# Moving the transposed adjacency of seven batches to its ring by DMA, and new orders on all five queues

## What is computed

```
v, q, k = relu(x Wv + bv), relu(x Wq + bq), relu(x Wk + bk)
att     = softmax((q k^T) * adj - 9e15 * (1 - adj))          # over the last axis
x1      = layernorm(x + relu((att v) Wo + bo))
h       = x1 W_w^T + W_b
u       = adj * exp((h a1)[:, None] + (h a2)[None, :] + a_b)
out     = layernorm(x1 + (u / sum(u)) h)
```

## Time and profile before

| | us |
|---|---|
| median of three runs | 395.15 (395.12 to 395.23) |
| the profiled execution | 395.13 |
| its span, first to last instruction | 393.4 |
| PE busy | 380.5 (97%) |
| ACT busy | 329.9 (84%) |
| DVE busy | 292.8 (74%) |
| POOL busy | 279.9 (71%) |

### The profile page before, as it was taken

The page is one execution under the profiler, slowest core; times in us unless marked ns, Lnnn a source line. Parts: engine busy times, 40 slices in busy tenths (PEclk is TensorE's granted clock), DMA queues, the critical chain, the costliest instruction groups (busy, mean ns, idle before and its releaser), DMA issues.

```text
span 393.4 us, 8653 instructions
## 1 busy us (share of the span) xinstructions
PE 380.5 (97%) x2757; PEld 355.2 (90%) x2757; DVE 292.8 (74%) x883; ACT 329.9 (84%) x661; POOL 279.9 (71%) x258
## 2 busy tenths in 40 slices
PE   8999999999999999999999999999999999999990
PEld 7798989989999999999999999999999999999990
DVE  3786796678668886777957887688867779697976
ACT  5877679987889887997879878898888969999962
POOL 1454951696458994789937998389956899576673
PEclk9999999999999999999999999999999999999996
DMA  8945533807657168754597266780676647978011
GB/s 259 376 166 166 164 129 137 328 38 268 200 185 314 61 235 260 262 203 171 175 292 298 84 240 215 243 322 13 253 214 233 252 162 285 386 224 282 4 55 53
DMA packets 38156, 80.71 MB, mean 205 GB/s; under 512 B 2785, under 2 KB 19681, under 8 KB 38113
## 3 DMA queue, kind: packets, MB, share of 16 engines
q1 hardware_dynamic: 37824, 80.03, 58.3%
q10 hardware_dynamic: 288, 0.14, 0.1%
HBM read 75.96 MB, written 4.19 MB: 204 GB/s over the span
## 4 chain that ended last, share of the span: by engine, by line
PE 91%; DVE 5%; issue 2%; POOL 0%; ACT 0%; POOLq 0%; DVEq 0%; ACTq 0%
PE pt_ps L1612 14%; PE m_ps L1660 13%; PE s_ps L1541 8%; PE av_ps L1625 8%; PE av_ps L1626 8%; PE av_ps L1624 8%; PE s_ps L1543 7%; PE s_ps L1542 7%; PE m_ps L1583 4%; PE m_ps L1649 3%; PE m_ps L1633 3%; PE m_ps L1541 2%; PE m_ps L1542 2%; PE m_ps L1543 2%; PE m_ps L1640 2%
## 5 line engine op out<-in xcount | busy, mean ns | idle before, releaser
L1033 DVE TENSOR_TENSOR prob_tl<-pt_ps,prob_th 128x512 fp32r<-128x512 f32 x128 | 85.5, 684 | 29.8 <-ACT prob_th L670 29.6
L1025 DVE CUSTOM_DVE_ANT_0 prob<-s_ps,penalty 128x1024 f32<-128x1024 f32 x64 | 78.0, 1218 | 30.8 <-PE s_ps L1543 26.2
L670 ACT ACTIVATE prob_th<-pt_ps 128x512 fp32r<-128x512 f32 x128 | 74.7, 596 | 21.0 <-PE pt_ps L1612 20.8
L405 POOL TENSOR_SCALAR penalty<-raw 128x1024 bf16<-128x1024 f32 x64 | 66.4, 1047 | 28.3 <-DMA raw<-in_adj_dram 13.2
L662 ACT ACTIVATE prob<-prob,neg_max 128x1024 f32<-128x1024 f32 x64 | 73.8, 1153 | 1.4 <-DVE neg_max L1025 1.3
L1624 PE MATMUL av_ps<-prob_th,vh 128*128 128x256 f32 x256 | 74.1, 290 | 0.0
L1612 PE MATMUL pt_ps<-rhs,prob 128*128 128x128 f32 x512 | 73.2, 273 | 0.0
L1626 PE MATMUL av_ps<-prob_th,vl 128*128 128x256 f32 x256 | 72.4, 283 | 0.0
L1625 PE MATMUL av_ps<-prob_tl,vh 128*128 128x256 f32 x256 | 72.4, 283 | 0.0
L607 ACT ACTIVATE adj_t<-adjt_in 128x1024 fp32r<-128x1024 f32 x56 | 59.3, 1061 | 11.2 <-PE m_ps L1660 11.1
L1612 PEld LDWEIGHTS pt_ps<-rhs,prob 128*128 128x128 f32 x512 | 60.1, 141 | 4.1
(11 more groups left out here) (139 smaller groups left out, 785.2 us busy)
## 6 DMA issues: line engine op xcount, KB each, us to landing
raw<-in_adj_dram SPq DMA_DIRECT2D x64, 512.0 KB, 5.6
adjt_in<-in_adj_t_dram SPq DMA_DIRECT2D x56, 512.0 KB, 3.9
x_in<-in_x_dram SPq DMA_DIRECT2D x8, 512.0 KB, 6.2
raw<-in_adj_t_dram SPq DMA_DIRECT2D x8, 512.0 KB, 5.7
out_dram<-out_sb SPq DMA_DIRECT2D x14, 256.0 KB, 4.5
xt_odd<-in_x_t_dram SPq DMA_DIRECT2D x8, 256.0 KB, 5.2
raw<-in_x_t_dram SPq DMA_DIRECT2D x7, 256.0 KB, 4.7
out_dram<-out_sb SPq DMA_DIRECT2D x4, 128.0 KB, 1.8
```

The lines of the kernel that those rows point to most:

```text
L670: sc.activation(prob_th[n % 2][:, tiles(k), (i % 2) * P:(i % 2 + 1) * P], pt_ps[k][:, :].rearrange("p (c n) -> p c n", n=P), ACT.Copy).the ...
L1025: v.tensor_tensor_reduce(out=prob[i % 2][:, :], in0=s_ps[:, :, :].rearrange("p a n -> p (a n)"), in1=penalty[:, n % RING, :], scale=-1.0, ...
L1033: v.tensor_tensor(prob_tl[n % 2][at], pt_ps[k][:, :].rearrange("p (c n) -> p c n", n=P), prob_th[n % 2][at].bitcast(F32), ALU.subtract).th ...
```

## The change

The transposed tiles of batches 0 to 6 are no longer copied from staging to ring by ACT. SP issues a DMA from the staging buffer to the ring buffer instead, behind a wait for the aggregate that frees the ring buffer and a wait for the tile's own load. Its end is what the aggregate and the next load into that staging buffer wait for, on one semaphore for each ring buffer. The bits are moved as they are. `round_adj` is gone from ACT's lists. All lists of the five queues have a new order, and so have the three lists of PSUM banks; no other step is added or left out. Of the orders those are shown that the text speaks of; in the rest only steps change places.

```diff
-        adjt_done = sem("adjt_done")
+        adjt_done = [sem(f"adjt_done{r}") for r in range(RING)]
...
             def load_adj_t(b, i):
                 n = T * b + i
-                wait(sp, adjt_done, n - STAGING + 1)
+                if n >= STAGING:
+                    sp.wait_ge(adjt_done[(n - STAGING) % RING], 16 * ((n - STAGING) // RING + 1))
                 sp.dma_start(adjt_in[:, n % STAGING, :, :], adj_t_tiles[b, i]).then_inc(adjt_arrived[n % STAGING], 16)
+
+            def copy_adj_t(b, i):
+                n = T * b + i
+                wait(sp, agg_full, n - RING + 1)
+                sp.wait_ge(adjt_arrived[n % STAGING], 16 * (n // STAGING + 1))
+                sp.dma_start(flat(adj_tile(b, i)).bitcast(F32), flat(adjt_in[:, n % STAGING, :, :])).then_inc(adjt_done[n % RING], 16)
 
...
             def head():
+                load_x_t(0, 1)
                 load_x_t_quarter(0)
                 load_x_t_quarter(1)
-                load_x_t(0, 1)
                 load_wb()
+                load_x_t(2, 0)
                 load_adj(0, 0)
+                load_x_t(1, 0)
                 load_adj(0, 1)
-                load_x(0)
-                load_x_t(1, 0)
-                load_x_t(1, 1)
...
             def batch_pass(p):
                 if there(p - 2):
+                    load_adj_t(p - 2, 6)
+                if there(p - 2):
                     load_adj_t(p - 2, 5)
+                if there(p - 2):
+                    copy_adj_t(p - 2, 6)
+                if there(p - 2):
+                    copy_adj_t(p - 2, 5)
                 load_adj(p, 4)
-                if there(p - 2):
-                    load_adj_t(p - 2, 6)
+                if there(p - 3):
+                    store(p - 3, 0)
                 load_adj(p, 5)
+                if there(p - 2):
+                    load_adj_t(p - 2, 7)
+                load_adj_t(p - 1, 0)
+                if there(p - 2):
+                    copy_adj_t(p - 2, 7)
+                if there(p + 2):
+                    load_x_t(p + 2, 1)
+                load_adj(p, 6)
+                load_adj_t(p - 1, 1)
+                copy_adj_t(p - 1, 0)
+                load_adj(p, 7)
+                load_adj(p + 1, 0)
+                load_adj_t(p - 1, 2)
+                copy_adj_t(p - 1, 2)
                 if there(p + 2):
                     load_x_t(p + 2, 0)
-                if there(p - 2):
-                    load_adj_t(p - 2, 7)
-                load_adj_t(p - 1, 0)
-                if there(p - 3):
-                    store(p - 3, 0)
-                if there(p + 2):
-                    load_x_t(p + 2, 1)
+                copy_adj_t(p - 1, 1)
+                load_adj_t(p - 1, 3)
+                load_adj(p + 1, 1)
                 if there(p - 3):
                     store(p - 3, 1)
-                load_adj_t(p - 1, 1)
+                copy_adj_t(p - 1, 3)
+                load_adj_t(p - 1, 4)
+                load_adj(p + 1, 3)
+                load_adj(p + 1, 2)
                 load_x(p + 1)
-                load_adj_t(p - 1, 2)
-                load_adj(p, 6)
-                load_adj(p, 7)
-                load_adj_t(p - 1, 3)
-                load_adj(p + 1, 0)
-                load_adj(p + 1, 1)
-                load_adj(p + 1, 2)
-                load_adj(p + 1, 3)
-                load_adj_t(p - 1, 4)
+                copy_adj_t(p - 1, 4)
 
...
             def batch_pass(p):
+                if there(p - 2):
+                    g_lo(p - 2, 0)
                 convert(p, 1)
                 if there(p - 2):
-                    g_lo(p - 2, 0)
-                if there(p - 2):
                     g_lo(p - 2, 1)
-                x_lo(p + 1, 0)
+                if there(p - 3):
+                    rstd1_pow(p - 3)
...
-            def round_adj(b, i):
-                n = T * b + i
-                wait(act, agg_full, n - RING + 1)
-                act.wait_ge(adjt_arrived[n % STAGING], 16 * (n // STAGING + 1))
-                sc.activation(flat(adj_tile(b, i)), flat(adjt_in[:, n % STAGING, :, :]), ACT.Copy).then_inc(adjt_done, 1)
...
             def head():
                 first_x_hi(0)
                 first_x_hi(1)
+                q_out(0, 0)
                 x_hi(0, 1)
-                q_out(0, 0)
                 k_out(0, 0)
+                v_relu(0, 0)
+                k_hi(0, 0)
                 q_hi(0, 0)
-                k_hi(0, 0)
                 k_out(0, 1)
+                v_relu(0, 1)
                 k_hi(0, 1)
+                v_relu(0, 2)
                 q_out(0, 1)
                 x_hi(1, 0)
...
             def head():
-                split_in(0)
                 first_x_lo_quarter(0)
                 first_x_lo_quarter(1)
+                split_in(0)
                 split_in(1)
+                centre_w()
+                v_bias(0, 0)
+                place_rhs1()
                 first_x_lo(1)
-                place_rhs1()
-                centre_w()
                 first_k_lo(0)
+                v_bias(0, 1)
                 first_q_lo(0)
-                v_bias(0, 0)
                 first_k_lo(1)
-                v_bias(0, 1)
+                v_bias(0, 2)
                 mask_max(0, 0)
-                v_bias(0, 2)
                 v_bias(0, 3)
                 v_bias(1, 0)
...
                 stats0_pair(2)
+                g_lo_pair(0)
+                stats1(LAST - 1, 0)
+                mean_var0_pair(2)
+                mean_var1(LAST - 1, 0)
+                inverse_sum_pair(3)
+                o_out(LAST, 3)
+                var_eps0_pair(2)
+                residual0(LAST, 3)
+                stats1(LAST - 1, 1)
                 shift0_pair(1)
-                mean_var0_pair(2)
-                stats1(LAST - 1, 0)
-                g_lo_pair(0)
-                mean_var1(LAST - 1, 0)
-                var_eps0_pair(2)
-                g_lo_den_pair(0)
-                stats1(LAST - 1, 1)
-                o_out(LAST, 3)
                 mean_var1(LAST - 1, 1)
-                residual0(LAST, 3)
+                var_eps1(LAST - 1)
...
                     pe.wait_ge(gl_done, 2 * (b + 1))
-                pe.wait_ge(adjt_done, n + 1)
+                pe.wait_ge(adjt_done[n % RING], 16 * (n // RING + 1))
...
                 first_project_q(0)
                 first_project_q(1)
                 project_k(0, 0)
+                project_v(0, 0)
+                project_v(0, 1)
                 project_k(0, 1)
                 project_q(0, 1)
-                project_v(0, 0)
                 form_w1()
-                project_v(0, 1)
+                project_v(0, 2)
                 first_scores(0)
                 first_scores(1)
-                project_v(0, 2)
                 project_v(0, 3)
                 project_v(1, 0)
+                project_v(1, 1)
                 scores(0, 1)
                 transpose_p(0, 0, 0)
...
             def batch_pass(p):
                 scores(p, 0)
                 transpose_p(p - 1, 7, 0)
+                if there(p - 2):
+                    aggregate(p - 2, 0)
                 transpose_p(p - 1, 7, 1)
                 project_out(p - 1, 1)
                 project_out(p - 1, 2)
                 scores(p, 1)
+                if there(p - 2):
+                    aggregate(p - 2, 1)
                 transpose_p(p, 0, 0)
                 transpose_p(p, 0, 1)
                 if there(p - 2):
-                    aggregate(p - 2, 0)
+                    aggregate(p - 2, 2)
                 attend(p - 1, 3)
+                if there(p - 2):
+                    aggregate(p - 2, 3)
                 scores(p, 2)
-                if there(p - 2):
-                    aggregate(p - 2, 1)
                 transpose_p(p, 1, 0)
+                if there(p - 2):
+                    aggregate(p - 2, 4)
                 project_out(p - 1, 3)
                 transpose_p(p, 1, 1)
                 project_q(p + 1, 0)
                 scores(p, 3)
                 project_k(p + 1, 0)
                 if there(p - 2):
-                    aggregate(p - 2, 2)
-                if there(p - 2):
-                    aggregate(p - 2, 3)
+                    aggregate(p - 2, 5)
+                project_v(p + 1, 0)
                 transpose_p(p, 2, 0)
-                project_v(p + 1, 0)
-                if there(p - 2):
-                    aggregate(p - 2, 4)
-                transpose_p(p, 2, 1)
-                scores(p, 4)
-                if there(p - 2):
-                    aggregate(p - 2, 5)
-                transpose_p(p, 3, 0)
                 if there(p - 2):
                     aggregate(p - 2, 6)
                 project_v(p + 1, 1)
+                scores(p, 4)
                 if there(p - 2):
                     aggregate(p - 2, 7)
+                transpose_p(p, 2, 1)
+                transpose_p(p, 3, 0)
                 attend(p, 0)
...
```

More of the change, by code:

```diff
@@ L953, in tail @@
-                round_last(6)
-                x1t_out_pair(1)
+                norm0_pair(0)
```

(16 more changed lines are left out.)

616 lines of the change are left out of this document (298 added, 318 removed), and 7 rows, old and new, of tables (HEAD_SLOTS, PASS_SLOTS).

## The result

The changed kernel takes 427.94 us (median of 4 runs, 425.57 to 429.95) against 395.19 us: a ratio of 1.083, interval 1.077 to 1.089. The forecast was 396.3 us and its range ended at 403.0: the side was right, the size was not. The profiled execution has a span of 428.1 us, 34.8 more than the 393.4 before.

The account below looks back on a forecast made before the run. PE's own stream was taken to bound the kernel from some 15 to some 370 us. 395.13 + 1.7 (head) - 0.5 (passes) + 0 (tail) = 396.3 us; its own range 394.0 to 398.5, with rivals 393.8 to 403.

Parts of the forecast that it names:

- What bounds the kernel: From some 15 to some 370 us PE's own stream, 46.2 us a pass, is the bound; ACT's rounding bounds nothing in the passes.
- The walk of SP's pass: SP's loads and copies in one pass, 3.2 us a landing: tile 7 lands 1.5 us before PE wants it; cost 0.
- The copy's own cost: Each 512 KB copy on SP's queue lands in 3.2 us and takes 1.4 us of the queues; DMA share 0.87.
- Copies bind: Rival, chance 0.18: copies in passes and tail take the queues 2.8 us each, making PE wait: 411 us, or 403.
- tile 7's chain: Four transfers between copy 5's issue and copy 7's landing in a pass: end at 25.6 instead of 21.7 at 2.8 us a copy.
- The rival of 411 us: Upper price of copies binding: tile 7 2.4 us late, six times in five passes and the tail, 14 us.
- the rival's lower price: Copies binding in the passes with tile 7 only 1 us late a pass: 403 us.
- The head: Before the passes, three moves delay PE's first product to about 6.1 us and the second scores to 15.75: +1.7, bounds +1.2 to +2.2.
- the passes' orders: In the passes, new orders win back part of PE's wait for `mask_max`: -0.5 us, bounds -0.9 and +0.5.
- the bound of 2.2 for a late clock: In the head, PE still at 1.2 GHz through `project_k(0, 0)` and v puts `mask_max(0, 0)` at 15.4: +2.2 us in all.
- Tail: Behind the last attend, the same steps in another turn: 0 us, bounds -1.4 and +0.7.
- ACT's busy time: Over the whole run, ACT's busy time falls to near 271 us as 56 roundings, 59.3 us, go.

Follow-up runs that it names:

- unlinked: The changed kernel, but every copy reads one tile that never changes and loads wait for no copy, with the same traffic: 404.3 us, ratio 1.023.
- staging4: The changed kernel with four staging buffers in place of two, so a load waits for a copy four tiles back: 408.2 us, ratio 1.033.
- hold2: The kernel before with 80 already met waits put into PE's list after aggregate 4 in each of five passes: 418.1 us, ratio 1.058.
- copies_alone: The kernel before without ACT's rounding, with SP's pass and tail lists of the changed kernel, copies included; other lists and head kept: 464.5 us, ratio 1.175.
- staging4_oldends: The changed kernel with four staging buffers, the old head, and the old last-batch lists on all engines but SP: 416.8 us, ratio 1.053.
- copy_on_act: The kernel before, orders and SP's list untouched, with each rounding replaced by a copy issued from ACT's own queue: 451.6 us, ratio 1.144.
- hold1: The kernel before with 40 already met waits put into PE's list after aggregate 4 in each of five passes: 399.6 us, ratio 1.012.
- staging4_oldhead: The changed kernel with four staging buffers and the head of the kernel before on all engines: 407.6 us, ratio 1.032.

## Why the prediction was wrong

**What bounds the kernel.** Right for the kernel before: PE's stream of 46.3 us a pass. ACT's rounding bounds nothing, and taking it away gave the passes nothing (46.5 in unlinked).

**The walk of SP's pass: the step that failed.** Its first half had the place right. It named tile 7 as the first to be late, with 1.5 us to spare, and tile 7 it is in all five passes. In pass 5, counted from 236.10, the walk's and the trace's landings are: copy 4 at 6.1 and 6.2, tile 5's load at 10.6 and 10.8, its copy at 13.9 and 14.8, tile 7's load at 18.5 and 20.7, its copy at 21.7 and 23.9. The second half was only sketched, as turns of load and copy for tiles 0 to 3 with landings to 41 us, and that was wrong by nearly 10: tile 3's copy landed at 50.5, and tile 4's load, which the next copy waits for, at 51.8. The mis-sized term is the landing. I took 3.2 us, the shortest of the earlier trace rows, where the median of the whole run is 3.9; copies range from 2.9 to 7.8 us, and the ten in the chain average 4.6. The four of the ten that were issued while a `load_adj` had 1 us or more to go took 5.2 to 6.5 us, the other six 3.2 to 4.3. Ten at 3.2 would have been 32 us of a 46 us pass; ten at 4.6, with issues, are 48.9. Ten at 3.9 would be, by the same count (an estimate), 42. So the added traffic has a part in the chain too: the median landing of this load went from 3.9 to 4.8 us. And I walked one pass and asked whether tile 7 made it. A round that is longer than the pass is late by more each time, until PE waits: that question, round against pass, I did not ask.

**The copy's own cost.** Right, and so the reason of the rival was wrong: 1.4 us of the queues taken, 1.34 measured, not 2.8. DMA share between 200 and 247 us was 0.81, and 0.87 in staging4, where the passes run on time; 0.87 was forecast. "Copies bind" was the case that came, at 0.18, by a mechanism that I had not priced: not bandwidth but latency in a row. It decided "from 1.5 us more than my walk", and the trace has 2.2 in pass 5. Its 25.6 us for tile 7's chain does not follow from its terms: 1.4 us more for each of the two copies among the four transfers make 24.5, for all four 27.3.

**The price of a stall.** Missing. The rival of 411 us put a stall at its own length, 2.4 us six times. In the changed kernel the waits were 20.3 us in nine places, and the clock went to 1.2 GHz four times, some 2 us more each; hold2 shows it alone. 28.1 us of waits and slow clock stand against the 14 of the rival. The range ended at 403, the rival's lower price, and left its worse half out.

**The head.** Mechanism right, size too small. First product at 6.31 (6.1 forecast), `project_k(0, 1)` at 9.81 (10.2), `scores(0, 1)` at 16.65 (15.75, or 16.3 with the slower clock). But alone it costs 5.0 us in the median of its runs, 2.3 to 5.7, not 1.7, and the bound of 2.2 for a late clock was too low: in the five profiles with the half pace `scores(0, 1)` stands 3.0 to 5.4 us later than before (in staging4, the 5.4, PE also waits 2.1 us for a load of x).

**The tail and the passes' orders.** Tail 0 forecast, with bounds of -1.4 and +0.7; behind the last attend it is +1.5, and it comes with the new lists of the last batch in all six kernels that have them. Which step of the tail was mis-sized stays open. Orders of the passes: -0.5 forecast, nothing won (46.5 in unlinked, 46.4 in staging4). ACT's busy time: 271 forecast by subtraction, 282 found. Busy time counts overlapping instructions once: the durations of ACT's instructions sum to 392.5 us before and 328.7 after, 63.8 less, but they overlap by 62.6 before and by 46.6 after. Nothing hung on it.

## What to carry to other kernels

When a compute step between two buffers becomes a transfer, its cost can be not its bandwidth but its landing in a chain: count the landings that follow one another in one round of the buffers, at the length that they have behind their neighbours on the queue, and hold that against the period of the engine that binds. If the round is longer, one or two more buffers may be worth more than all care for the list: here they gave back 16 and 20 us. Another order of SP's list for two buffers was not tried. A list in which each wait holds up the rest has to be made together with the order of the engine that it feeds (copies_alone, staging4_oldends). And a stall of some 3 us on PE is to be priced with the slow clock behind it.

## What the runs showed of the hardware

- A 512 KB transfer from SBUF to SBUF by DMA landed in 2.9 us at best, 4.2 in the median and 7.8 at most in the changed kernel, and took all 16 engines for 1.34 us in copy_on_act. The loads of the same size from HBM landed in 3.1, 4.8 and 8.3 us in the changed kernel: moving within SBUF was hardly quicker.
- What is still out at the issue of a copy lengthens it: in the changed kernel copies landed in 3.5 us on average with no other transfer out (7 copies), 3.6 with one (20), 4.4 with two (18), 5.8 with three (10).
- PE's clock: gaps of 0.9 us (hold1), of 1.45 and 2.30 us (the changed kernel, passes 2 and 3) and one of 2.92 us (copies_alone, to 109.44) left it at 1.00. The five gaps of 3.0 to 3.2 us (hold2) were each followed by 3.4 us at 0.50, the three of 3.8 to 4.1 us (the changed kernel) by 3.4 or 6.8 us, and so was one of 2.36 us (staging4_oldhead, 0.50 from 373.26 to 376.67). In the head an idle stretch of 1.6 to 1.8 us was followed by either pace (products of 256 columns 0.11 or 0.21 us apart).
- Waits that are already met are cheap on PE but not free: 40 of them made a gap of 0.9 us, 80 one of 3.2.
